# A macaron block with its engines' orders made anew: beta folded into the FFN bias, the norm's halves split straight from PSUM, and an order of its own for each phase

## What is computed

```python
x = x + 0.5 * ffn(layernorm(x));  x = x + attn(layernorm(x));  x = x + 0.5 * ffn(layernorm(x))
def ffn(x):    # layernorm again, with gamma and beta, then a ternary weight
    xn = (x - mu) * rsqrt(var + 1e-5) * gamma + beta
    return einsum('bsi,oi->bso', xn, clip(round(w / (mean(abs(w)) + 1e-5)), -1, 1)) + bias
def attn(x):   # 16 query heads, 4 key and value heads of 128; causal, window of 64
    q, k, v = rope(x @ Wq + bq), rope(x @ Wk + bk), x @ Wv + bv
    return softmax(mask(q @ k.T / sqrt(128))) @ v @ Wo + bo
```

## Time and profile before

| | |
|---|---|
| median of 3 runs | 871.69 us (868.89 to 873.82) |
| the profiled execution | 871.4 us, span 869.6 |
| TensorE busy | 794.8 us, 91% of the span |
| VectorE, ScalarE, GpSimd busy | 650.1 (75%), 502.1 (58%), 461.7 (53%) |
| prologue up to K0n | 34.55 us |
| middle phases, six | 147.42 to 752.89 us |
| last phase, epilogue | 91.28 and 25.39 us |

### The profile page before, as it was taken

How to read it: one execution, slowest core, us unless ns; L and a number is a source line. 1 busy time by engine, 2 the same in 40 slices (tenths; PEclk the granted TensorE clock), 3 DMA queues, 4 the chain that set the end, 5 groups by cost and what they waited for, 6 DMA issues and landing times.

```text
span 869.6 us, 16025 instructions
## 1 busy us (share of the span) xinstructions
PE 794.8 (91%) x5638; PEld 735.4 (85%) x5638; DVE 650.1 (75%) x1233; ACT 502.1 (58%) x1595; POOL 461.7 (53%) x527
## 2 busy tenths in 40 slices
...
DMA packets 52431, 70.53 MB, mean 81 GB/s; under 512 B 7040, under 2 KB 30080, under 8 KB 52352
## 3 DMA queue, kind: packets, MB, share of 16 engines
...
...
## 4 chain that ended last, share of the span: by engine, by line
DVE 30%; PE 30%; ACT 17%; issue 7%; POOL 6%; DMA 6%; SPq 4%; POOLq 0%; DVEq 0%; ACTq 0%
PE job_p L543 10%; ACT probs L847 9%; PE attn_p L543 7%; DVE rope_sin L729 6%; DMA rope_swap<-rope_sin 5%; DVE rope_cos L734 5%; PE scores_p L560 4%; DVE probsT L705 4%; DVE neg_max L687 4%; DVE headsT L699 4%; PE heads_p L543 3%; ACT headsT L869 3%; ACT y L890 3%; PE probsT_p L600 2%; POOL q_s L955 2%
## 5 line engine op out<-in xcount | busy, mean ns | idle before, releaser
L847 ACT ACTIVATE probs<-scores_p,neg_max 128x128 f32<-128x128 f32 x512 | 180.5, 364 | 225.0 <-DVE neg_max L687 225.0
L955 POOL TENSOR_TENSOR q_s<-rope_cos,rope_swap 128x512 f32<-128x512 f32 x128 | 165.2, 1291 | 154.7 <-DMA rope_swap<-rope_sin 151.1
L543 PE MATMUL attn_p<-wo_s,headsT 128*128 128x256 f32 x1536 | 210.5, 286 | 11.0 <-DVE headsT L699 10.9
L543 PE MATMUL job_p<-xnT,wq_s 128*128 128x512 f32 x768 | 209.1, 408 | 7.4 <-DVE v_s L739 7.2
L543 PEld LDWEIGHTS attn_p<-wo_s,headsT 128*128 128x128 f32 x1536 | 194.5, 191 | 17.6 <-DVE headsT L699 13.8
L941 POOL TENSOR_TENSOR probs<-probs,inv_sum 128x512 f32<-128x512 f32 x128 | 133.3, 1041 | 77.7 <-DVE inv_sum L693 77.7
L543 PEld LDWEIGHTS job_p<-xnT,wq_s 128*128 128x128 f32 x768 | 138.2, 192 | 33.9 <-DVE v_s L739 9.1
L699 DVE SCALAR_TENSOR_TENSOR headsT<-heads_p,columns_s,headsT 128x512 fp32r<-128x512 f32 x128 | 95.7, 748 | 81.4 <-ACT headsT L869 81.0
L560 PE MATMUL scores_p<-k_s,q_s 128*128 128x128 f32 x1024 | 134.9, 275 | 0.1
L560 PEld LDWEIGHTS scores_p<-k_s,q_s 128*128 128x128 f32 x1024 | 129.4, 191 | 6.4 <-POOL q_s L955 0.6
L729 DVE SCALAR_TENSOR_TENSOR rope_sin<-job_p,columns_s,rope_t 128x512 f32<-128x512 f32 x160 | 118.7, 742 | 11.1 <-PE job_p L543 10.7
...
## 6 DMA issues: line engine op xcount, KB each, us to landing
...
```

The lines of the kernel that those rows point to most:

```text
L543: mm = nc.tensor.matmul(dst, a(p), b(q), start=first and clears and i == 0, stop=last and i == 2, skip_group_check=True)
L847: ins = nc.scalar.activation(probs[:, i, k, :], scores_p[i][:, k, :], ACT.Exp, bias=neg_max[:, i, k:k + 1], accum_out=row_sum[:, i, k:k + 1])
L955: nc.gpsimd.tensor_tensor(roped(x), as_roped(x, rope_cos[:, r, :]), as_roped(x, rope_swap[:, r, :]), ALU.add).then_inc(rope_added, 1)
```

## The change

Beta leaves the norm: xn * W + bias with xn = z * gamma + beta is z * gamma * W + (beta * W + bias). TensorE makes beta * W once (beta), VectorE folds it into half_b. YT's halves then come straight from PSUM, ScalarE's with gamma as its scale, VectorE's in one operation; lnT is double and ln_full is gone (w_full holds the FFN weight). The variance's term and the negated mean move from GpSimd to VectorE. Each phase may have a table of its own. Low halves of weight pieces 3 to 7 move to GpSimd, constants are issued by ScalarE's queue instead of SyncE's.

```diff
-TENSOR = """
-    K1c Q4c
-    S0c O13p W14p T15p
-    S1c Q5c V10c O14p W15p T0c Q6c
-    S2c Q7c O15p W0c YT0p T1c
-    S3c K2c Q8c O0c W1c T2c Q9c
-    S4c O1c W2c V11c T3c
-    S5c FO0p YT1p O2c W3c Q10c T4c Q11c
-    S6c O3c W4c T5c FO1p K3c
-    S7c YT0n O4c W5c T6c Q12c
-    S8c O5c FO0n W6c YT1n T7c Q13c
-    S9c Q14c O6c W7c FO1n T8c
-    S10c Q15c XT0n O7c W8c T9c
-    S11c XT1n O8c W9c T10c K0n
-    S12c Q0n O9c W10c T11c
-    S13c Q1n V00n O10c W11c T12c
-    S14c Q2n O11c W12c T13c Q3n
-    S15c V01n O12c W13c T14c
-"""
-VECTOR = """
-    heads13p probsT14p K1c Q4c max0c evac0p stats0p heads14p probsT15p inv0c max1c
-    Q5c w8f inv1c heads15p V10c Q6c probsT0c max2c Q7c evac1p inv2c
-    stats1p YT0p heads0c probsT1c K2c max3c Q8c end_YT0p heads1c probsT2c inv3c
-    Q9c max4c stats0n tern0i tern1i inv4c stats1n heads2c V11c probsT3c max5c
-    FO0p YT1p inv5c heads3c Q10c end_YT1p probsT4c Q11c w9f max6c inv6c
-    FO1p heads4c probsT5c K3c max7c YT0n inv7c heads5c end_YT0n Q12c probsT6c
-    max8c w0i FO0n astats0n YT1n heads6c Q13c probsT7c end_YT1n inv8c Q14c
-    max9c heads7c w1i FO1n inv9c astats1n probsT8c max10c Q15c inv10c heads8c
-    probsT9c w2i w3i w4i XT0n max11c XT1n inv11c heads9c probsT10c w5i
-    w6i w7i K0n max12c Q0n inv12c heads10c probsT11c max13c Q1n inv13c
-    V00n heads11c probsT12c max14c Q2n inv14c heads12c probsT13c Q3n max15c inv15c
-    V01n
-"""
-SCALAR = """
-    probsT14p w8f exp0c heads14p probsT15p mask2c norm0p exp1c mask3c heads15p V10c
-    probsT0c exp2c mask4c heads0c probsT1c YT0p norm1p exp3c heads1c probsT2c mask5c
-    w9f exp4c heads2c mask6c V11c probsT3c exp5c norm0n heads3c YT1p mask7c
-    probsT4c exp6c heads4c probsT5c mask8c norm1n exp7c heads5c w0i YT0n probsT6c
-    mask9c exp8c heads6c probsT7c mask10c w1i YT1n w2i anorm0n heads7c exp9c
-    probsT8c mask11c exp10c anorm1n heads8c probsT9c w3i w4i XT0n mask12c XT1n
-    w5i w6i w7i exp11c heads9c probsT10c mask13c exp12c mask14c heads10c probsT11c
-    exp13c V00n mask15c heads11c probsT12c exp14c mask0n heads12c probsT13c exp15c V01n
-    mask1n heads13c
-"""
-GPSIMD = """
-    K1c scale0p probs0c Q4c bias0p probs1c Q5c Q6c probs2c Q7c scale1p
-    bias1p K2c Q8c probs3c scale0n probs4c Q9c scale1n probs5c half0i bias0n
-    Q10c Q11c probs6c residual0c probs7c bias1n K3c Q12c ascale0n Q13c probs8c
-    Q14c probs9c ascale1n probs10c Q15c probs11c K0n probs12c Q0n probs13c Q1n
-    probs14c Q2n Q3n probs15c
-"""
-SYNC = """
-    load0c K1c Q4c Q5c stage9f Q6c Q7c K2c Q8c Q9c shift1c
-    store0p Q10c Q11c store1p K3c Q12c Q13c Q14c Q15c stage8i K0n
-    Q0n Q1n Q2n Q3n shift0n
-"""
+TENSOR = {
+    "prologue": """
+    total0i YT0n beta0i YT1n FO0n FO1n open0i XT0n XT1n K0n Q0n Q1n Q2n Q3n
+    V00n V01n
+    """,
+    "first": """
+    K1c Q4c S0c Q5c S1c Q6c V10c T0c S2c Q7c W0c T1c S3c K2c
+    Q8c O0c W1c T2c Q9c V11c S4c O1c W2c T3c S5c Q10c O2c W3c
+    T4c Q11c S6c O3c W4c T5c K3c YT0n S7c O4c W5c T6c Q12c S8c
+    O5c YT1n W6c T7c Q13c FO0n S9c O6c W7c Q14c FO1n T8c Q15c O7c
+    XT0n W8c S10c T9c S11c XT1n O8c W9c T10c K0n S12c Q0n O9c W10c
+    T11c S13c V00n Q1n O10c W11c T12c S14c Q2n O11c W12c T13c Q3n S15c
+    V01n O12c W13c T14c
+    """,
+    "middle": """
+    K1c Q4c O13p S0c W14p T15p Q5c S1c O14p W15p V10c Q6c T0c S2c
+    Q7c YT0p O15p W0c T1c K2c S3c O0c Q8c W1c YT1p T2c S4c Q9c
+    O1c FO0p W2c T3c Q10c S5c V11c O2c W3c T4c S6c Q11c FO1p O3c
+    W4c YT0n T5c S7c K3c O4c W5c T6c S8c Q12c YT1n O5c W6c Q13c
+    T7c S9c FO0n Q14c FO1n O6c W7c T8c S10c Q15c XT0n O7c W8c T9c
+    S11c XT1n O8c W9c K0n T10c O9c Q0n S12c W10c Q1n T11c S13c O10c
+    V00n W11c T12c S14c Q2n O11c W12c T13c S15c Q3n V01n O12c W13c T14c
+    """,
+    "epilogue": """
+    O13p W14p T15p O14p W15p O15p YT0p YT1p FO0p FO1p
+    """,
+...
+VECTOR = {
+    "prologue": """
+    stats0n tern0i stats1n tern1i beta0i YT0n YT1n FO0n astats0n FO1n astats1n w2i w0i XT0n
+    XT1n w1i K0n Q0n Q1n Q2n Q3n V00n V01n
+    """,
+    "middle": """
+    heads13p probsT14p K1c Q4c max0c evac0p heads14p stats0p probsT15p inv0c max1c Q5c inv1c V10c
+    Q6c heads15p max2c probsT0c Q7c evac1p stats1p heads0c inv2c YT0p probsT1c K2c max3c Q8c
+    heads1c YT1p stats0n inv3c probsT2c Q9c max4c heads2c FO0p inv4c Q10c max5c probsT3c V11c
+    inv5c heads3c max6c probsT4c Q11c FO1p inv6c stats1n heads4c probsT5c max7c YT0n K3c max8c
+    heads5c probsT6c Q12c inv7c YT1n heads6c Q13c max9c FO0n inv8c probsT7c Q14c astats0n FO1n
+    astats1n inv9c heads7c max10c probsT8c Q15c XT0n heads8c max11c probsT9c inv10c XT1n heads9c probsT10c
+    inv11c K0n max12c Q0n heads10c Q1n inv12c probsT11c max13c heads11c max14c inv13c probsT12c Q2n
+    inv14c V00n heads12c max15c Q3n inv15c probsT13c V01n
+    """,
+    "epilogue": """
+    heads13p probsT14p evac0p heads14p probsT15p stats0p heads15p evac1p stats1p YT0p YT1p FO0p FO1p
+    """,
+}
+SCALAR = {
+    "prologue": """
+    norm0n norm1n YT0n YT1n w1i w3i w0i w2i anorm0n anorm1n XT0n XT1n mask0n V00n
+    w5i V01n mask1n w4i
+    """,
+    "middle": """
+    probsT14p heads14p exp0c probsT15p mask2c exp1c V10c heads15p probsT0c norm0p mask3c exp2c YT0p heads0c
+    probsT1c norm1p mask4c heads1c YT1p probsT2c exp3c mask5c heads2c exp4c probsT3c V11c mask6c exp5c
+    heads3c probsT4c mask7c exp6c norm0n heads4c YT0n mask8c probsT5c norm1n exp7c probsT6c heads5c exp8c
+    YT1n mask9c heads6c probsT7c mask10c exp9c heads7c probsT8c anorm0n XT0n anorm1n mask11c heads8c probsT9c
+    exp10c XT1n mask12c heads9c exp11c mask13c probsT10c heads10c exp12c probsT11c mask14c V00n heads11c exp13c
+    probsT12c exp14c mask15c heads12c mask0n probsT13c exp15c mask1n V01n heads13c
+    """,
+    "epilogue": """
+    probsT14p heads14p probsT15p heads15p norm0p YT0p norm1p YT1p
+    """,
+}
+GPSIMD = {
+    "prologue": """
+    scale0n half0i scale1n bias0n bias1n ascale0n ascale1n w3i K0n Q0n Q1n Q2n Q3n w5i
+    """,
+    "first": """
+    w4f probs0c K1c probs1c Q4c Q5c probs2c Q6c Q7c probs3c w6f K2c scale0n w7f
+    probs4c scale1n Q8c probs5c bias0n Q9c Q10c probs6c Q11c residual0c probs7c K3c bias1n probs8c
+    ascale0n Q12c Q13c ascale1n probs9c Q14c probs10c Q15c probs11c probs12c probs13c K0n Q0n probs14c
+    Q1n Q2n probs15c Q3n
+    """,
+    "middle": """
+    K1c probs0c scale0p probs1c Q4c Q5c Q6c bias0p scale1p Q7c probs2c probs3c bias1p probs4c
+    scale0n K2c Q8c Q9c probs5c probs6c Q10c scale1n Q11c residual0c bias1n probs7c K3c bias0n
+    Q12c probs8c ascale0n Q13c ascale1n probs9c Q14c probs10c Q15c probs11c K0n probs12c Q0n probs13c
+    probs14c Q1n Q2n Q3n probs15c
+    """,
+}
+SYNC = {
+    "prologue": """
+    K0n Q0n Q1n Q2n Q3n shift0n stage8i
+    """,
+    "first": """
+    load0n K1c Q4c Q5c stage9f Q6c Q7c K2c shift1c Q8c Q9c Q10c Q11c K3c
+    Q12c Q13c Q14c Q15c K0n Q0n Q1n Q2n Q3n shift0n
+    """,
+    "middle": """
+    K1c Q4c Q5c load0n Q6c Q7c K2c Q8c Q9c Q10c shift1c Q11c store1p store0p
+    K3c Q12c Q13c Q14c Q15c K0n Q0n Q1n Q2n Q3n shift0n
+    """,
+}
 class Phase: ...                      # Phase, Tally: replaced by
+def numbered(steps, *kinds):
+    return {x: n for n, x in enumerate(x for x in steps if x[0] in kinds)}
...
+            def beta_product(_):
+                pe.wait_ge(tern_ready, 1)
+                for e in range(EC):
+                    mm = nc.tensor.matmul(attn_p[0][:, 0, :], beta_s[:, e:e + 1].to_broadcast([P, P]),
+                                          w_tern[:, e, :].bitcast(F32), start=e == 0, stop=e == EC - 1)
+                mm.then_inc(beta_ready, 1)
...
+            def fold_beta(_):
+                nc.vector.scalar_tensor_tensor(out=half_b, in0=attn_p[0][:, 0, :], scalar=0.5, in1=half_b,
+                                               op0=ALU.mult, op1=ALU.add).then_inc(bias_ready, 1)
...
+            def ffn_in_high(x):
+                for e in range(EC):
+                    ins = nc.scalar.activation(lnT[:, r, 0, e, :], bank[:, e * 2 * P:(e + 1) * 2 * P], ACT.Copy,
+                                               scale=gamma_s[:, e:e + 1])
+            def ffn_in_low(x):
+                for e in range(EC):
+                    ins = nc.vector.scalar_tensor_tensor(
+                        out=lnT[:, r, 1, e, :], in0=bank[:, e * 2 * P:(e + 1) * 2 * P], scalar=gamma_s[:, e:e + 1],
+                        in1=lnT[:, r, 0, e, :].bitcast(F32), op0=ALU.mult, op1=ALU.subtract)
...
+                nc.vector.tensor_scalar(variance[:, half], stats[:, half, 1], factor, added, ALU.mult,
+                                        ALU.add).then_inc(moments_ready, 1)
+                nc.vector.tensor_scalar(minus_mean[:, half], stats[:, half, 0], -1.0, None,
+                                        ALU.mult).then_inc(moments_ready, 1)
...
+                for n in (2, 8, 9):          # residual, first phase
+                    wait_split(pool, n)
```

(24 more changed lines are left out.)

745 lines of the change are left out of this document (382 added, 363 removed).

## The result

The changed kernel takes 818.89 us, median of 4 runs (817.5 to 819.94), against 871.51 (868.89 to 873.82) of the kernel before beside it: ratio 0.9396 [0.9364, 0.9428], 52.6 us faster.

What follows compares the result with a forecast made beforehand. TensorE was taken to bound the middle, with looser ends; savings of 8.4 + 1 + 5.5 + 18 + 4 + 2.7 = 39.6 us took 871.4 to 831.8, or 832 against the median; range 818 to 853.

Steps and rivals of the forecast that it cites:

- the middle comes to its floor: Rival, chance 0.12: middle phases save 4.7 us each, 28 in all, and the ends 25, giving 819 us.
- bound from the floor: Middle phases: only about 4.7 us a phase above TensorE's fixed work can be won, 28 us in all.
- The middle: Six middle phases: removed TensorE waits save a net 3.0 us a phase, 18 in all, bounds 0 to 28.
- The 0.8 given back: Middle phases: 0.8 us a phase set against the saving for possible new lateness at XT0n, O9c and T7c.
- T0c's and Q7c's waits: Middle phases: waits of 1.93 and 1.38 us in the phase shown, traced to K1c's late add, would go.
- T8c's wait: Middle phases: 1.21 us waiting for probs8c behind ascale0n and Q13c on GpSimd, would go with the new order.
- New work at nothing: Middle phases: YT's new halves, moved moments and longer-held banks cost nothing, being covered, as neither ScalarE nor VectorE is the bound.
- the second cover: Steps ahead of the second reuse of a YT bank in a middle phase: 4.4 us new, 2.6 before.
- The slow rival: Rival, chance 0.05: YT banks released late, 6.2 us or more after, stall TensorE two jobs behind each YT; 888 us.
- First phase: From S0c to the first phase's end: of 9.0 us idle and about 2 hidden, 5.5 saved (2 to 8.5).
- the 1.5 that I gave back: First phase: 1.5 us set against the saving because T1c inherits the late K1c add.
- Prologue: Up to K0n: YT0n ahead of the bank opening and halves run as a wave save 8.4 us (5 to 11).

Runs made afterwards that it cites:

- before_fixed: Kernel before with three moves: x loads behind Q5c's swap, probabilities ahead of the scale, exp1c and V10c ahead of norm0p and heads15p; 851.95 us.
- bank_held: Kernel before, but YT's bank is freed when the low half is made, not at the scaling, with end_YT0p one step earlier; 939.88 us.
- old_split: Changed kernel with its new orders, but YT's old three steps (scale into a full tile, copy, subtract) put back, beta still folded; 841.13 us.
- constants_sync: Changed kernel with the five constant loads issued by SyncE again; 817.79 us, ratio 0.9391.
- best2: Changed kernel with constants on SyncE, early table load, splits held back, second staged weight before prologue swaps, first-phase x loads behind Q5c; 810.80 us.

## Why the prediction was right, and where it was short

The side was right, and the range (818 to 853) with 0.9 us to spare; the likeliest value was 13 us too high, and its own range (824 to 842) was missed. What came is the case called "the middle comes to its floor", at 819, to which I gave 0.12: its 28 us for the middle measured 29.5, and its 25 for the ends 25.1. The list of waits and their causes was right, and its sum stopped short; that the range still held is owed to the bound from the floor.

**The middle, the mis-sized term.** I took 3.0 us a phase, 18 in all. It measured 4.9 and 29.5. Two steps were off. The 0.8 given back did not come: none of the three places named (XT0n, O9c, T7c) waits in the middle of the changed kernel. And the small rest (hidden idle time, the waits of a few tenths) went too, which I had left for the upper bound of 28. The mechanism of the counted part holds: before_fixed, which takes away the causes of T0c's and Q7c's waits alone, has middle phases of 98.4 us, 2.5 less than before; T8c's wait is still in it. My bound from the floor, 4.7, was right within 0.2; I put it in the range and too little of the chance on it.

**New work at nothing.** Right for this kernel, and the part where the case was nearest to going wrong. "Neither engine is the bound" doesn't carry it: with the old orders the same operations cost 28 us, and the longer hold of the bank by itself 69. Cover and hold together carry it. Recounted, the second cover is 4.1 us in the new order, where I wrote 4.4, and 4.0 in the old, where I wrote 2.6. So that place gained no cover, and what saved it was a hold of 2.5 us, which I had not worked out: for all four places I took one release, of 6.2 us and more, where 2.5 to 5.6 were measured. In bank_held the holds went beyond the covers of the old order at three places, with waits of 2.0 to 3.2 us. The slow rival had its place and mechanism right, but named a price without the clock: the phase shown lost 1.6 us more for each of its three waits. And the sum lacked the other side: under the new orders the split from PSUM is worth 22 us (14 in the middle), where it takes a step out of YT's chain and some 0.8 us of VectorE out of each YT (0.87 for 1.7). Which single step loses old_split's 2.4 a phase was not taken apart.

**First phase**, 8.5 for 5.5: T0c's 5.23 went as read from the earlier trace rows; W0c's 0.73 and T1c's 0.84 are the 1.5 that I gave back. Of the 8.5, 6.8 are idle time and 1.7 TensorE's busy time, a term that the sum did not have. Behind T0c's wait the kernel before ran at a low clock, and the changed kernel's first phase has 1.00 throughout:

```profile
61.49:65.00 3.51, 3.51 (x13) 2.98 (x14) 0.02 (x1) 0.60 (x1) 3.40 (x3) 0.57 0.00 0
```

The profiled execution was also a good one for this phase: the kernels with the same first table lay 1.5 to 3.4 us above it.

**Prologue**, 7.5 for 8.4, near by errors that cancel. YT0n came 2.6 late, since x landed 2.9 later with the constants issued beside it. The matmuls then ran faster than forecast: both FO in some 2.4 us and not 4, the opening 1.88 and not 3.7. The power beside the split took 1.59 us (1.60 in constants_sync, beside the same split), where the others in these prologues take 0.69 to 0.73, so the collision was real, and the opening did not cover it: XT1n waited 2.57. The Trainium skill, SBUF — State Buffer, section Who interferes with whom, says that a VectorE instruction with two SBUF inputs contends with a GpSimd one that reads SBUF; the pair at 21.14 and 21.32 agrees, and best2, which holds the splits back, shows 0.69.

**K0n to S0c**, 0.3 for 1: K0n takes 2.90 us in both kernels, behind idle time in both, and in the kernel before no step of this stretch waits, so the splits were not in the way. **Last phase** and **epilogue**, 4.9 for 4 and 3.8 for 2.7: as described. In the last phase a late unit now takes 3.99 us, with a wait of 0.23 for heads, where two of those before waited 1.00; W, heads, O is the chain that is left.

Of what I said would show it: K0n at 27.0 (26 forecast), T0c 6.1 us behind S0c (6), no wait for probabilities over 1 us in the middle, YT1p directly behind YT0p. Middle phases of 98 was the miss.
